# A two-layer graph network with experts on one Trainium2 core: the second routing keeps its rows in token order, and the experts find their tokens by table search

## The reference

```python
x = x + _L1_ffn_ref(_layernorm(x), Wg, bg, W1, b1, W2, b2)   # x [6250, 256]

def _L1_ffn_ref(xf, Wg, bg, W1, b1, W2, b2):                 # E = 8, D = 256, H = 1024
    # the two largest of softmax(xf @ Wg + bg), scaled to sum 1, are the token's shares
    for e in range(E):
        h = gelu(xf @ W1[e] + b1[e])
        out = out + w_dense[:, e:e + 1] * (h @ W2[e] + b2[e])
```

## Time and profile before

| what | us |
|---|---|
| median of 3 runs | 2768.6 (2764.55 to 2768.83) |
| profiled execution, its span | 2768.1 |
| gate stage with the wait behind it | 1926.3 to 2081.1 |
| last experts' stage | 2081.1 to 2768.1 |

### The profile page before, as it was taken

How to read it: one execution, slowest core, us unless ns; L and a number is a source line. 1 busy time by engine, 2 the same in 40 slices (tenths; PEclk the granted TensorE clock), 3 DMA queues, 4 the chain that set the end, 5 groups by cost and what they waited for, 6 DMA issues and landing times. The chain is left out here.

```text
span 2768.1 us, 56379 instructions
## 1 busy us (share of the span) xinstructions
PE 2069.7 (75%) x13133; PEld 1854.5 (67%) x13134; DVE 1559.2 (56%) x4220; ACT 975.2 (35%) x2748; POOL 1480.2 (53%) x1459
## 2 busy tenths in 40 slices
PE   4423218988376788788888888787808999999997
PEld 3323218988355666666666666665708999999997
DVE  4566525655575666666656566666714555555543
ACT  2333216766241111111111111112305656665664
POOL 2167653434106777777777777775672343334323
PEclk9755559999786888888888787878558999999999
DMA  7312243333354444444444444444642333333331
GB/s 188 84 51 79 73 121 103 114 86 108 121 188 106 115 113 113 112 114 113 110 111 112 111 112 111 112 108 105 199 134 72 67 77 45 73 69 69 69 49 22
DMA packets 204140, 279.41 MB, mean 101 GB/s; under 512 B 74634, under 2 KB 158197, under 8 KB 203953
## 3 DMA queue, kind: packets, MB, share of 16 engines
q0 software_dynamic: 82480, 201.42, 27.9%
q1 hardware_dynamic: 120841, 76.64, 10.6%
q10 hardware_dynamic: 776, 0.89, 0.1%
HBM read 202.11 MB, written 78.46 MB: 101 GB/s over the span
## 5 line engine op out<-in xcount | busy, mean ns | idle before, releaser
L1737 POOL DMA_INDIRECT at_G<-h_as,at_idx x850 | 808.9, 952 | 389.9 <-issue 262.4
L1941 PE MATMUL at_pAgg<-at_G,at_OH 128*128 128x260 f32 x1700 | 549.1, 492 | 133.8 <-DVE at_ACC L1789 92.0
L1941 PEld LDWEIGHTS at_pAgg<-at_G,at_OH 128*128 128x128 f32 x1700 | 413.9, 250 | 234.3 <-DVE at_G L1771 149.3
L1262 POOL DMA_INDIRECT out_dram<-e_ob,e_to x108 | 172.8, 1600 | 404.0 <-DMA out_dram<-e_ob,e_to 190.4
L1454 ACT ACTIVATE e_full<-e_pH,g_bias_hidden 128x256 f32<-128x256 f32 x640 | 326.2, 510 | 110.6 <-PE e_pH L1359 92.7
L1881 ACT ACTIVATE at_OT<-at_pTr 128x384 f32<-128x384 f32 (+1 forms) x300 | 125.7, 470 | 668.0 <-PE at_pTr L1926 667.7
L1535 DVE TENSOR_TENSOR e_hT_low<-e_full,e_hT_high 128x256 fp32r<-128x256 f32 x536 | 259.8, 498 | 110.3 <-ACT e_hT_high L1455 109.5
L1357 PE MATMUL e_pH<-e_xT_high,e_WA_high 128*128 128x256 f32 x1072 | 309.7, 289 | 6.4 <-DVE e_WA_low L1530 4.3
L1358 PE MATMUL e_pH<-e_xT_low,e_WA_high 128*128 128x256 f32 x1072 | 304.2, 284 | 0.0
L1359 PE MATMUL e_pH<-e_xT_high,e_WA_low 128*128 128x256 f32 x1072 | 304.1, 284 | 0.0
L1771 DVE TENSOR_TENSOR at_G<-at_G,at_pIds 128x1536 f32<-128x1536 f32 x150 | 249.9, 1666 | 87.6 <-ACT at_pIds L1888 87.6
(11 more groups left out here) (332 smaller groups left out, 3825.8 us busy)
## 6 DMA issues: line engine op xcount, KB each, us to landing
e_xs<-slot_rows_e SPq DMA_DIRECT2D x55, 261.0 KB
e_xs<-slot_rows_e SPq DMA_DIRECT2D x54, 257.0 KB
at_G<-h_as,at_idx POOLq DMA_INDIRECT x850, 2.8
b_rows<-expert_out SPq DMA_DIRECT2D x14, 896.0 KB, 7.2
g_raw_first<-in_L_ffn_W_dram POOLq DMA_DIRECT2D x8, 1024.0 KB, 8.2
g_raw_last<-in_L_ffn_W_dram POOLq DMA_DIRECT2D x8, 1024.0 KB, 6.4
xt_ar<-a_og SPq DMA_DIRECT2D x7, 910.0 KB, 4.4
h_as<-b_og SPq DMA_DIRECT2D x7, 910.0 KB
```

The source lines that it names most:

```text
L1262: gp.indirect_dma_start(K.out, at, ob[b][:, s, :], None, bounds_check=NODES - 1, oob_is_err=False, compute_op=ALU.add).then_inc(sent[s], 16)
L1737: gp.indirect_dma_start(G[j][:, c, :], None, K.T1, bass.IndirectOffsetOnAxis(ap=idx[j][:, c:c + 1], axis=0)).then_inc(gathered[j], 16)
L1941: last = nc.tensor.matmul(pAgg[:, 0:DIM + 4], OH[j][:, c, :], G[j][:, c, :], start=(j == 0 and c == 0), stop=(j == NJ - 1 and c == CHUNKS[ ...
```

## The change

A new stage, `gating()`, takes the place of `project(..., gate=...)`. It writes each tile's rows in token order to `gate_rows` (SP, seven plain transfers); a row is 256 features and eight shares, one for each expert, zero where the token does not go. Nothing is scattered and no slot is computed. Instead DVE keeps a table of who goes where (`PAIRS`, 128 tokens x 8 experts x 49 tiles, held twice), and PE and DVE make from it at the end, for each expert, `SPAN` (the rank of the first token of each node tile and of the one behind it) and `LOOK` (the running count of tokens within each node tile). The stage is written out without loops, the activation tables stay loaded, and `x` goes to the output in two transfers.

In the last experts' stage each slot tile now searches for its 256 tokens, five tiles ahead (`AHEAD = 5`). `tile_spans` (DVE) marks for each slot the node tile it falls in, `look_up` (PE, two products over 98 rows) fetches that tile's running counts into free columns of the `pO` banks, `find` (DVE) counts how many are below the slot's rank and so has the token, `hand` (DVE) passes the numbers on, and `gather` (POOL, two indirect DMAs of 128 rows) fetches the rows. SP loads nothing there any more. `shares` becomes one copy.

```diff
@@ gate stage
-        project(K, "b1", None, gate=(L1_ffn_Wg, L1_ffn_bg))
+        gating(K, L1_ffn_Wg, L1_ffn_bg)
+                for i in range(TRIPS):
+                    a = i * BODY
+                    sp.wait_ge(routed, i + 1)
+                    sp.dma_start(K.ROWS[a * P:(a + BODY) * P, :].rearrange("(t p) c -> p t c", p=P), Y[:, a:a + BODY, :]).then_inc(rows_out, 16)
...
+                ch.mark(V.scalar_tensor_tensor(K.LOOK[:, :, 0:P], pC[0:2 * TILES, :, :], K.half[:, 0:1],
+                                               base[:, :].rearrange("p (e o) -> p e o", o=1).to_broadcast([2 * TILES, E, P]), ALU.mult, ALU.add))
...
+                for e in range(E):
+                    last = nc.tensor.matmul(pC[0:2 * TILES, e, :], K.PAIRS[:, e, :], K.upto[:, :], start=True, stop=True)
@@ experts, POOL
+                def gather(t, b, rows):
+
+                    gp.wait_ge(rows_found, t + 1)
+                    if not isinstance(t, int) or t >= 2:
+                        freed(gp, to_ready, t - 1)
+                    gp.sem_inc(passed, 1)
+                    for s in range(SUB):
+                        gp.indirect_dma_start(xs[b][:, s, :], None, K.ROWS, bass.IndirectOffsetOnAxis(ap=rows[:, s:s + 1], axis=0)).then_inc(x_in[b], 16)
+
+                if not deep:
+                    gather(0, 0, first_rows[0])
+                    gather(1, 1, first_rows[1])
                 split_last(0)
...
+                    with gp.Fori(0, last) as i:
+                        for b in range(2):
+                            trip(i, b)
+                            gather(i * 2 + (b + AHEAD), (b + AHEAD) % 2, rows_of[(b + AHEAD) % 2])
@@ experts, PE
+                        for at, n in searches:
+                            if u == at:
+                                look_up(n, n % 2 if isinstance(n, int) else b)
...
-                def final(t, b):
+                def final(t, b, searching):
...
+                    if searching:
+                        pe.wait_ge(find_done, t + (AHEAD + 1))
...
+                def look_up(t, b):
+
+                    e = expert(pe, t)
+                    pe.wait_ge(tile_of_ready, t + 1)
+                    if not isinstance(t, int):
+                        pe.wait_ge(find_done, t)
+                        freed(pe, scaled_ready, (t - AHEAD) * SUB)
+                    elif t > 0:
+                        pe.wait_ge(find_done, t)
+                    for s in range(SUB):
+                        last = nc.tensor.matmul(pS[:, s, :], tile_of[b][:, s * P:(s + 1) * P],
+                                                K.LOOK[:, bass.ds(e, 1), 0:P + 1].rearrange("p o n -> p (o n)"), start=True, stop=True)
+                    last.then_inc(looked_up, 1)
...
-                        first(r + D, (b + D) % 2)
+                        early = [(2 * n + 1, n + 2) for n in range(AHEAD - 2)] if not deep and begin and not end else []
+                        first(r + D, (b + D) % 2, [(HC // 2 - 1, r + AHEAD)] if searching else early)
@@ experts, DVE
+                def tile_spans(t, b):
+
+                    at = slice(t, t + 1) if isinstance(t, int) else bass.ds(t, 1)
+                    ch = Chain(v, spanned, t * 2)
+                    e = expert(v, t)
+                    ch.link(V.tensor_scalar(limits[:, :], K.SPAN[:, bass.ds(e, 1), :].rearrange("p o k -> p (o k)"),
+                                            K.RANK0[0:2 * TILES, at], None, ALU.subtract))
+                    ch.link(V.tensor_scalar(reached[:, :], K.slot[0:2 * TILES, :], limits[:, 0:1], None, ALU.is_ge))
+                    V.scalar_tensor_tensor(tile_of[b][:, :], K.slot[0:2 * TILES, :], limits[:, 1:2], reached[:, :], ALU.is_lt, ALU.mult).then_inc(tile_of_ready, 1)
+                    v.wait_ge(tile_of_ready, t + 1)
+
+                def find(t):
+
+                    at = slice(t, t + 1) if isinstance(t, int) else bass.ds(t, 1)
+                    ch = Chain(v, search, t * (SUB + 1))
+                    v.wait_ge(looked_up, t + 1)
+                    for s in range(SUB):
+                        ch.mark(V.tensor_scalar(lower[:, s, :], pS[:, s, 0:P], K.RANK0[:, at], K.token[:, s:s + 1], ALU.subtract, ALU.is_le))
+                    ch.settle()
+                    ch.link(V.tensor_reduce(place[:, :].rearrange("p (s o) -> p s o", o=1), lower[:, :, :], AX.X, ALU.add))
+                    V.scalar_tensor_tensor(found[:, :], pS[:, :, P], float(NODEROWS), place[:, :], ALU.add, ALU.add).then_inc(find_done, 1)
+                    v.wait_ge(find_done, t + 1)
...
                     if end:
                         o_out(r, b)
-
+                    if searching:
+                        tile_spans(r + (AHEAD + 1), (b + AHEAD + 1) % 2)
...
+                if not deep:
+                    tile_spans(0, 0)
+                    for t in range(2):
+                        tile_spans(t + 1, (t + 1) % 2)
+                        find(t)
+                        hand(t, first_rows[t])
                 v.wait_ge(W.biases, 16 * W.n_biases)
                 lows("a", 0)
```

More of the change, by code:

```diff
@@ L959, in deviations @@
                         nc.scalar.activation(z[:, :, :], z[:, :, :], ACT.Exp).then_inc(exps_done, 1)
-                    if not gate:
-                        act.wait_ge(stats_ready, i + 1)
+                    act.wait_ge(stats_ready, i + 1)
                     nc.scalar.activation(std[:, :, :], mv[:, :, 1:2], ACT.Sqrt, bias=K.eps[:, 0:1]).then_inc(std_ready, 1)
-                def shares(n):
-                    act.wait_ge(gap_in, n)
-                    nc.scalar.activation(gap[:, :, :], gap[:, :, :], ACT.Exp).then_inc(gap_out, 1)
                 deviations(0)
@@ L1001, in _ @@
                             take(j - 1)
-                        if gate and j == BODY - 3:
-                            with act.If(i > 0):
-                                shares(i)
-                        if j == BODY - 2 and not gate:
+                        if j == BODY - 2:
                             with act.If(i < TRIPS - 1):
@@ L1013, in _ @@
                         take(BODY - 1)
-                if gate:
-                    shares(TRIPS)
                 if router:
@@ L1191, in experts @@
         x_high = sem("x_high")
-        x_in = [sem(f"x_in{b}") for b in range(2)]
+        x_in = [sem(f"x_in{b}", software=not deep) for b in range(2)]
+        XIN = 16 if deep else 16 * SUB
         to_ready = sem("to_ready")
@@ L1369, in turn, with first @@
                     last.then_inc(pX_ready, 1)
-                def first(t, b):
+                def first(t, b, searches):
                     e = expert(pe, t)
@@ L1571, in trip @@
                     r = i * 2 + b
+                    searching = not deep and begin and begin != "last" and end
                     if begin and begin != "last":
```

444 lines of the change are left out of this document (340 added, 104 removed).

## The result

The changed kernel takes 2831.57 us (median of 4 runs, 2830.08 to 2836.49) against 2767.77 us before: the ratio is 1.0238, with a 95% interval of 1.0223 to 1.0252. It is slower, by 64 us. Its profiled execution has a span of 2829.1 us, 61.0 us above the 2768.1 of the one before.

The account below looks back on a forecast made before the run. It took POOL's scatter tail to bound the hole before the experts' stage and PE the experts' loop. Gate stage and lead-in -56, period +73, split +34 and gathers +12 gave +63 on 2768.1: 2831 us, range 2775 to 2880.

Parts of the forecast that it names:

- the loop closed by the change: Last experts' stage: final to final through scale, tile_spans, look_up and find; period 13.6 us where PE alone needs 11.84 to 12.0.
- The three terms of the loop: From final(0) to final(52): +73 us for the longer period, +34 at changes of expert, +12 for late gathers.
- the split: At seven changes of expert, POOL's splitting of output weights delays DVE's work on the loop: +34 us (0 to 34).
- the gathers: POOL's gathers stand behind late scatters at a change of expert and land late for turn: +12 us (0 to 30).
- The shared port: At changes of expert, POOL's instruction holds the port pair exclusively and fully blocks DVE, making its lows 4.4 us late.
- Gate stage: Routing before the last experts' stage: scatters and slot positions go, tables take 11.3 us; experts' stage starts 70.4 us earlier.
- The end of the hole: Before the experts' stage: after POOL issues its last scatter, some 11 us pass until it lands and the barrier opens.
- Lead-in: Experts' stage up to final(0): first search, gathers and three early searches add 14.4 us (+5 to +24).
- (a): Experts' loop: the search hides in DVE's idle time, period 12.3 us, 2719 us in all; chance 0.14.
- (b): Experts' loop: POOL's scatters and gathers become the bound, period 12.9 us, 2795 us in all; chance 0.07.
- (c): Experts' loop: TensorE's clock falls to a mean near 0.95 through PE's pauses, +31 us, 2862 in all; chance 0.07.
- The tail: What follows final(52), 28.7 us before the change, was forecast to be unchanged.

Follow-up runs that it names:

- spans_first: Changed kernel with DVE's tile_spans put ahead of o_out instead of behind it; loop 741.3 us against 750.1, ratio to the kernel before 1.0086.
- no_split: Changed kernel with POOL splitting only 4 of 256 columns of later experts' output weights; loop 710.9 us against 750.1, ratio to the kernel before 1.0012.
- gather_first: Changed kernel with POOL's two gathers ahead of everything else in its trip; loop 739.2 us against 750.1, ratio to the kernel before 1.0126.
- three: Changed kernel with tile_spans ahead of o_out, look_up after the second unit, find after the third low, gathers first; 2731.4 us, ratio to before 0.9883.
- look1_alone: Changed kernel with look_up after the second unit and find after the third low, tile_spans left behind o_out; loop 795.5 us, ratio to before 1.0414.
- spans_twice: Changed kernel with the first two operations of tile_spans done twice in place; loop 795.4 us against 750.1, ratio to the kernel before 1.0325.
- scatter98: Changed kernel with POOL writing the gate stage's rows by 98 indirect DMAs (two copies) in place of SP's seven transfers; ratio to before 1.0388.
- scatter49: Changed kernel with POOL writing the gate stage's rows by 49 indirect DMAs (one copy) in place of SP's seven transfers; ratio to before 1.0191.

## Why the prediction was right, point by point

**What bounds the kernel, and the loop closed by the change.** Right in mechanism and size: the period was put at 13.6 us, and the 35 intervals under 14 us have 13.62 on average. Each link of the chain can be laid beside the row above: final to scale 6.22, measured 6.23; `tile_spans` 1.9 with the read, measured 1.4 to the end of `e_tile_of`, then 0.13 or 0.56 to `x_out`; PE's wait at `look_up` about 1 us, measured 0.5 to 0.7; at `final` 0.5, measured 0.3 or 0.5. One link was right by luck: five lows at 0.4 us hold only because DVE comes to them late. spans_first showed that ACT's chain lies 0.3 us below, which the prediction did not see and which would have mattered had `tile_spans` been cheaper.

**The three terms of the loop** gave +119 and the loop took +117. Ordinary tiles: 51 x 13.62 + 11.7 = 706, +73, as the term. The other 44 us came at the changes of expert. The prediction counts them above ordinary tiles, and so can the trace: the seven intervals of 17.9 to 18.6 us are 30.8 above it, where the split was put at 34, and the nine behind them 13.1, where the gathers were put at 12. The experiments agree: no_split takes away 39.2, with the late gathers that follow from the split in it, and gather_first 10.8; the two overlap and are not to be added.

**The shared port.** The lows were not the only operations held up. `e_limits`, two elements, took 0.69 us and ended with POOL's copy (2214.2); `e_reached`, which reads a single SBUF tensor, took 2.45 us instead of 0.29 beside POOL's subtraction. The section that the prediction cites, "SBUF: two separate sides" of the Trainium skill's "SBUF — State Buffer", names beside operations with two SBUF inputs an operation of VectorE in a two-port mode; the rows agree with it if these two ran in such a mode, which the trace does not name. `x_out`, with one operand in PSUM, took its usual 0.69 us beside POOL's second subtraction.

**Gate stage**: -70.4 forecast, -74.0 measured, inside its bounds. The end of the hole was read wrongly (the landing takes 2.7 us and POOL's DRAIN 8.2), without effect on the sum, since neither stands at the stage's end once the scatters are gone. Trips were faster than thought (8.7 us from the logits of one to the next, not 8.9, and 8.3 between their `b_Y`), and the tables took 10.3 us, not 11.3. **Lead-in**: +14.4 forecast, +17.4 measured, inside its bounds. The first search and the gathers, put at 9.0 us, took 7.4 up to PE's first transposes; the three early searches, put at 5.4, are the term that was too small, with 10.1 us from there to `final(0)`, of which PE's two stops are 8.1. The two errors, -3.6 of the gate stage and +3.0 of the lead-in, nearly cancel: that the sum comes within 2 us of the measured span is in part luck.

**The rivals.** (a) did not happen, and three shows what it takes: three edits and a period of 12.12, at 2731 us. (b) is excluded by the same kernel. (c) played a small part in the changed kernel: the clock is 0.97 over the loop, full in ordinary tiles, and falls at every change of expert behind PE's wait of 3.8 us, where it is nearly hidden six times out of seven, and in three intervals behind such changes, where it costs 1.5 us each. It played a real one in look1_alone. The tail's +2.0 us was not foreseen: POOL's last instruction, again a DRAIN, takes 5.97 us where it took 4.35, and starts 24.4 us after `final(52)`, not 24.1.

## What to carry to other kernels

When work is put into a pipeline, ask for each wait that it adds which instruction released it, and follow that back until you come to the instruction you started from. If you do, you have a period, and its length has nothing to do with how busy the engines are. Place the pieces so that each stands where its engine waits anyway, and move them together: here one edit alone gave 9 us, another alone cost 45, and the set gave 98.

An engine's disturbance (here POOL's split) has no price of its own; it costs what the chain it hits has no slack for, 8 us, 17 or 39.

## What the runs showed of the hardware

POOL's 2.34 us subtraction held up an operation of DVE that reads one bf16 tensor (`e_reached`, 0.29 to 2.45 us), and its copy of 1.04 us one of two float32 elements (`e_limits`, 0.23 to 0.69), not only those with two SBUF operands; `x_out`, with one operand in PSUM, was not held up (0.69 us with and without). Where a scatter of POOL's had begun 0.6 us before `e_reached`, it took some 0.5 us and not 0.29 (spans_twice).

The clock was full in ordinary tiles of the changed kernel, where PE pauses 0.5 us at `look_up` and 0.3 or 0.5 at `final`. With one pause of 2.0 us a tile it fell in about every third tile, which cost 1.5 us there, and its mean over the loop was 0.95 (look1_alone). Behind a wait of 3.8 us at `look_up` it fell each of seven times.

POOL's DRAIN at the end of a stage took 8.2 us behind 98 indirect writes (before, scatter98) and 4.2 behind 49 (scatter49). And with indirect writes from POOL under way, the other engines of the written-out gate stage were slower, though none of their trips waits for the writes: one trip took 20 us with 98 of them and 12.3 with 49, not 8.3 (scatter98, scatter49), for a reason that is still open.
